# Linear-attention layers of a fused four-stack transformer: whole layers written out, and the second MLP layer moved by one pass

## The reference, cut to what matters

```python
for i in range(8):                       # layers
    residual = x
    Q  = _feature_map(einsum('nsd,hdk->nshk', x, Wq[i]) + bq[i])   # elu(.) + 1
    Kf = _feature_map(einsum('nsd,hdk->nshk', x, Wk[i]) + bk[i])
    V  = einsum('nsd,hdk->nshk', x, Wv[i]) + bv[i]
    KV, sumK = sum(Kf * V, axis=1), sum(Kf, axis=1)
    Z = 1.0 / (Q * sumK[:, None] + 1e-06)
    att = (Q * KV[:, None] * Z).reshape(n, s, 16 * 64)
    x = _layer_norm(gelu(att @ Wo[i] + bo[i]) + residual, ln1_s[i], ln1_b[i])
    residual = x
    h = gelu(x @ W1[i] + b1[i])          # 128 -> 512
    h = gelu(h @ W2[i] + b2[i])          # 512 -> 128
    x = _layer_norm(h + residual, ln2_s[i], ln2_b[i])
```

## Time and profile before

| | |
|---|---|
| median of three runs | 5932.04 us |
| lowest, highest | 5924.21, 5944.2 us |
| profiled execution, its own time | 5937.09 us |
| its span, first to last instruction | 5935.3 us |
| busy over the span: TensorE, VectorE, ScalarE, GpSimd | 80%, 64%, 50%, 19% |
| the linear-attention layers in it | from 1393 to about 4318 us |
| TensorE's mean granted clock | 0.893 of full speed |

### The profile page before, as it was taken

One profiled execution on the slowest core, in us unless ns is written; L12 is line 12 of the kernel. 1 busy time (PEld: TensorE's weight loads), 2 busy tenths in 40 slices (PEclk: granted clock), 3 DMA queues, 4 the chain that ended last, 5 costly groups with the idle time before them and its releaser, 6 DMA issues.

```text
span 5935.3 us, 74341 instructions
## 1 busy us (share of the span) xinstructions
PE 4747.4 (80%) x19788; PEld 2813.9 (47%) x19788; DVE 3781.6 (64%) x11596; ACT 2983.3 (50%) x5234; POOL 1115.9 (19%) x1520
## 2 busy tenths in 40 slices
PE   4778888866888888888888888888858745999964
PEld 2667777753333333333333333333335533666643
DVE  4445554467776767667666776777665674556576
ACT  1010000015887878778787787878712212555531
POOL 1100000021222222222222222222220002333310
PEclk9888888878999999999999999999979966989976
DMA  1000000000000000000000000000000000110100
GB/s 47 1 1 1 1 1 1 1 1 18 0 15 4 6 13 1 15 4 10 9 1 18 0 11 7 1 18 0 0 0 0 0 0 22 37 40 35 43 1 14
DMA packets 96397, 59.02 MB, mean 10 GB/s; under 512 B 58809, under 2 KB 91278, under 8 KB 93604
## 3 DMA queue, kind: packets, MB, share of 16 engines
q1 hardware_dynamic: 88436, 42.52, 2.7%
q10 hardware_dynamic: 7600, 12.58, 0.6%
HBM read 46.49 MB, written 8.61 MB: 9 GB/s over the span
## 4 chain that ended last, share of the span: by engine, by line
PE 49%; DVE 24%; issue 12%; ACT 8%; DMA 2%; POOL 1%; DVEq 1%; ACTq 1%; SPq 1%; POOLq 0%
PE bank L1493 7%; PE bank L1526 4%; PE bank L1507 4%; PE bank L1215 3%; DVE arena L1657 3%; DVE arena L1643 3%; PE bank L1520 3%; PE bank L2163 3%; PE bank L1212 3%; DVE arena L1626 2%; PE bank L1204 2%; DMA packed_dram<-arena 2%; DVE arena L1282 2%; DVE arena L1668 2%; PE bank L2196 2%
## 5 line engine op out<-in xcount | busy, mean ns | idle before, releaser
L1493 PE MATMUL bank<-arena 128*128 (+1 forms) x3072 | 1478.9, 619 | 12.9 <-ACT arena L1555 11.3
L1493 PEld LDWEIGHTS bank<-arena 128*128 128x128 f32 x3072 | 601.2, 200 | 745.4 <-issue 713.1
L1626 DVE SCALAR_TENSOR_TENSOR arena<-arena 128x256 f32<-128x256 f32 x1024 | 390.5, 418 | 777.7 <-ACT arena L1555 773.1
L1507 PE MATMUL bank<-arena 128*128 128x512 f32 x1024 | 565.4, 635 | 219.6 <-DVE arena L1657 218.2
L1568 ACT ACTIVATE arena<-arena,const_table 128x256 f32<-128x256 f32 x1024 | 558.6, 600 | 78.7 <-POOL arena L1695 78.6
L1695 POOL TENSOR_SCALAR arena<-arena 128x512 f32<-128x512 f32 x512 | 317.9, 621 | 1353.9 <-DVE arena L1637 1346.6
L1643 DVE SCALAR_TENSOR_TENSOR arena<-bank,bv,arena 128x256 f32<-128x256 f32 x1024 | 450.0, 476 | 0.0
L1657 DVE SCALAR_TENSOR_TENSOR arena<-arena 128x256 f32<-128x256 f32 x1024 | 447.6, 478 | 0.7 <-issue 0.7
L1507 PEld LDWEIGHTS bank<-arena 128*128 128x128 f32 x1024 | 168.6, 191 | 556.3 <-DVE arena L1657 499.2
L1554 ACT ACTIVATE arena<-bank,bqk 128x512 f32<-128x512 f32 x512 | 350.3, 684 | 159.5 <-PE bank L1493 126.2
L1637 DVE SCALAR_TENSOR_TENSOR arena<-bank,bqk,arena 128x512 f32<-128x512 f32 x512 | 384.1, 750 | 18.0
(11 more groups left out here) (350 smaller groups left out, 8804.6 us busy)
## 6 DMA issues: line engine op xcount, KB each, us to landing
arena<-packed_dram SPq DMA_DIRECT2D x48, 192.0 KB
arena<-packed_dram ACTq DMA_DIRECT2D x16, 576.0 KB
arena<-in_L_attn_Wk_dram SPq DMA_DIRECT2D x16, 256.0 KB, 3.2
arena<-in_L_attn_Wq_dram SPq DMA_DIRECT2D x16, 256.0 KB, 3.9
arena<-in_L_attn_Wv_dram SPq DMA_DIRECT2D x16, 256.0 KB, 4.4
arena<-in_L_attn_Wo_dram SPq DMA_DIRECT2D x8, 512.0 KB, 3.8
arena<-in_L_attn_W_dram SPq DMA_DIRECT2D x16, 256.0 KB, 3.0
packed_dram<-arena SPq DMA_DIRECT2D x16, 192.0 KB, 2.1
```

Source lines behind the costliest of these rows:

```text
L1493: nc.tensor.matmul(bank[:, RING1[m % 5], :], w1p[k][:, i * P:(i + 1) * P], zT_of(g), start=True, stop=True).then_inc(a1_proj.sem, 1)
L1507: nc.tensor.matmul(bank[:, 6, :], wo1[:, i, :], a1_att[:, i % 4, :], start=(i == 0), stop=(i == NB1 - 1)).then_inc(a1_outd.sem, 1)
L1626: last = nc.vector.scalar_tensor_tensor(seqs(a1_kf[:, i % 2, :])[q], seqs(a1_ek[:, i % 2, :])[q], 1.0, seqs(a1_kf[:, i % 2, :])[q], ALU.mi ...
```

## The change

In `over_layers` the loop over pairs of slots goes: all eight slots of a layer are written out, the loop over layers 1 to 7 stays, `opening` is left once a layer, and the drain has three slots. There are four hooks, in slots 0 to 3: the biases of y, of h and x1, and of h2 and ln2 are copied apart. W1 and W2 are loaded apart, each when its own last product is done.

The MLP is cut in two. `h_pe` (lag 2, at w = 3) makes the four products with W1 into banks 0, 1, 6 and 0. The products with W2 (`h2_pe`) go to the next slot (lag 3), two at w = 0 and two at w = 1, into bank 1; their gelu `h2_act` (lag 3) is the first of the gelu window, which is now at w = 3. The second norm has lag 3 with its steps at w = 4 to 6, the first norm has its transposes in at w = 5, statistics at w = 6, normalisation at w = 7 and its transposes back in the next slot at w = 0 (lag 2).

`out_pe`, `inv_act` and `att_dve` come one block later (w - 4, w - 2, w - 3), `query_pool` stands at w, and gpsimd sums the second residual ahead of the first. `a1_ek`, `a1_eq`, `a1_kf` have three buffers, `a1_x1` two, and `a1_fin` shares the memory of `a1_h`.

```diff
     def one_layer(layer, low):
         parts = parts_of(layer)
         opening()
-        for s in range(2):
-            hooks[s](layer)
+        for s in range(G):
+            if s < len(hooks):
+                hooks[s](layer)
             slot(parts, s, low, G)
-        hooks[2](layer)
-        with eng.Fori(0, (G - 2) // 2) as j:
-            opening()
-            for v in range(2):
-                for lag, fn in parts:
-                    fn(2 * j + (2 + v - lag), (v - lag) % 2)
...
+            HBANK = (0, 1, 6, 0)
...
                             a1_y_act.wait(nc.tensor, t - 1)
-                            a1_h2_act.wait(nc.tensor, t - 2)
+                            if not before_all(g, 2):
+                                a1_h_act.wait(nc.tensor, t - 2, 3)
...
-                def mlp_pe(g, u):
+                def h_pe(g, u):
                     t = turn(g)
+                    nc.tensor.wait_ge(a1_w1_loaded, 16 * weights_of(g))
                     a1_x1d.wait(nc.tensor, t)
                     for i in range(NF1):
+                        if i == 1:
+                            a1_h2_act.wait(nc.tensor, t - 1)
+                        if i == 2:
+                            if isinstance(g, int) and g == G - 1:
+                                a1_y_act.wait(nc.tensor, t)
+                            else:
+                                a1_y_act.wait(nc.tensor, t + 1)
+                        if i == 3:
+                            a1_h_act.wait(nc.tensor, t, 1)
+                        nc.tensor.matmul(bank[:, HBANK[i], :], w1a[:, i * P:(i + 1) * P], a1_x1[:, u, :],
                                          start=True, stop=True).then_inc(a1_h_psum.sem, 1)
...
+                def h2_pe(half):
+                    def fn(g, u):
+                        t = turn(g)
+                        if half == 0:
+                            nc.tensor.wait_ge(a1_w2_loaded, 16 * weights_of(g))
+                            a1_h_act.wait(nc.tensor, t)
+                            a1_zt.wait(nc.tensor, t - 1)
+                        for i in range(half * NF1 // 2, (half + 1) * NF1 // 2):
+                            last = nc.tensor.matmul(bank[:, 1, :], w1b[:, i, :], a1_h[:, i, :],
+                                                    start=(i == 0), stop=(i == NF1 - 1))
...
                 for w in range(NB1):
                     pe.append((0, proj_pe(w)))
-                    of(pe, out_pe, w - 3)
+                    of(pe, out_pe, w - 4)
                     act.append((0, exp_act(w)))
-                    of(act, inv_act, w - 1)
+                    of(act, inv_act, w - 2)
                     dve.append((0, feature_dve(w)))
-                    of(dve, att_dve, w - 2)
-                    of(pool, query_pool, w - 1)
-                    if w == 2:
-                        pe.append((2, mlp_pe))
-                        act += [(1, gelu_table_act), (1, y_act), (2, h_act), (1, exp_table_act)]
-                        pool += [(1, residual_pool(0)), (2, residual_pool(1))]
+                    of(dve, att_dve, w - 3)
+                    of(pool, query_pool, w)
+                    if w == 0:
+                        pe += [(2, turn_back_pe(0)), (3, h2_pe(0))]
+                        act.append((2, back_act(0)))
+                    if w == 1:
+                        pe.append((3, h2_pe(1)))
                     if w == 3:
-                        pe += [(1, turn_in_pe(0)), (2, turn_in_pe(1))]
-                        dve += [(1, norm_stats_dve(0)), (2, norm_stats_dve(1))]
+                        pe.append((2, h_pe))
+                        act += [(1, gelu_table_act), (3, h2_act), (1, y_act), (2, h_act), (1, exp_table_act)]
+                        pool += [(3, residual_pool(1)), (1, residual_pool(0))]
                     if w == 4:
-                        pool += [(1, norm_rstd_pool(0)), (2, norm_rstd_pool(1))]
+                        pe.append((3, turn_in_pe(1)))
+                        dve.append((3, norm_stats_dve(1)))
+                        pool.append((3, norm_rstd_pool(1)))
                     if w == 5:
-                        dve += [(1, norm_dve(0)), (2, norm_dve(1))]
+                        pe.append((1, turn_in_pe(0)))
+                        dve.append((3, norm_dve(1)))
                     if w == 6:
-                        pe += [(1, turn_back_pe(0)), (2, turn_back_pe(1))]
-                        act += [(1, back_act(0)), (2, back_act(1))]
+                        pe.append((3, turn_back_pe(1)))
+                        act.append((3, back_act(1)))
+                        dve.append((1, norm_stats_dve(0)))
+                        pool.append((1, norm_rstd_pool(0)))
+                    if w == 7:
+                        dve.append((1, norm_dve(0)))
```

More of the change, by code:

```diff
@@ L39 @@
 C_ALL = C_HEAD + 16
-ARENA = 25728
+ARENA = 26752
 def host_table():
@@ L159, in over_layers @@
     opening()
-    for s in range(G, G + 2):
+    for s in range(G, G + 3):
         slot(parts, s, 0, G)
@@ L1464, in one_layer @@
                     if not first:
+                        a1_h_psum.wait(sp, layer * G - 1)
+                    sp.dma_start(w1a[:], one("W1").rearrange("l d f -> d (l f)")).then_inc(a1_w1_loaded, 16)
+                    if not first:
                         a1_h2_psum.wait(sp, layer * G - 1)
-                    sp.dma_start(w1a[:], one("W1").rearrange("l d f -> d (l f)")).then_inc(a1_mlp_loaded, 16)
                     sp.dma_start(w1b[:], one("W2").rearrange("l (b p) d -> p (l b) d", p=P))\
-                        .then_inc(a1_mlp_loaded, 16)
+                        .then_inc(a1_w2_loaded, 16)
                 if n:
@@ L1509, in out_pe, with weights_of, before_all @@
                     return fn
-                def mlp_pe(g, u):
+                def weights_of(g):
+                    return layer if isinstance(g, int) and g < 0 else layer + 1
+                def before_all(g, back):
+                    return isinstance(layer, int) and layer == 0 and isinstance(g, int) and g < back
+                def h_pe(g, u):
                     t = turn(g)
-                    before = isinstance(g, int) and g < 0
-                    nc.tensor.wait_ge(a1_mlp_loaded, 32 * (layer if before else layer + 1))
+                    nc.tensor.wait_ge(a1_w1_loaded, 16 * weights_of(g))
@@ L1530, in turn_in_pe @@
                 def turn_in_pe(i):
                     def fn(g, u):
-                        lns[i]["in"].wait(nc.tensor, turn(g))
+                        t = turn(g)
+                        lns[i]["in"].wait(nc.tensor, t)
+                        if i == 0 and not before_all(g, 1):
+                            a1_h_act.wait(nc.tensor, t - 1)
+                        if i == 1 and not (isinstance(g, int) and g == G - 1):
+                            a1_h_act.wait(nc.tensor, t + 1, 2)
                         for q in range(QT):
@@ L1592, in h_act, with h2_act @@
                             a1_h2_psum.wait_free(nc.scalar, t)
-                        nc.scalar.activation(a1_h[:, i, :], bank[:, i % 2, :], ACT.Gelu_apprx_tanh,
+                        nc.scalar.activation(a1_h[:, i, :], bank[:, HBANK[i], :], ACT.Gelu_apprx_tanh,
                                              bias=b11[:, i:i + 1]).then_inc(a1_h_act.sem, 1)
+                def h2_act(g, u):
+                    t = turn(g)
                     a1_h2_psum.wait(nc.scalar, t)
-                    lns[1]["in"].wait_free(nc.scalar, t)
-                    nc.scalar.activation(a1_g2[:], bank[:, 6, :], ACT.Gelu_apprx_tanh, bias=bd1[:, 3:4])\
+                    lns[1]["in"].wait(nc.scalar, t - 1)
+                    nc.scalar.activation(a1_g2[:], bank[:, 1, :], ACT.Gelu_apprx_tanh, bias=bd1[:, 3:4])\
                         .then_inc(a1_h2_act.sem, 1)
```

71 lines of the change are left out of this document (38 added, 33 removed).

## The result

| | before | after |
|---|---|---|
| median (lowest to highest) | 5928.5 us (5924.21 to 5944.2) | 5870.38 us (5866.52 to 5872.23) |
| ratio, 95% interval | | 0.9896 (0.9877 to 0.9916) |
| profiled execution, its span | 5937.09, 5935.3 us | 5872.23, 5870.4 us |
| TensorE's mean granted clock | 0.893 | 0.901 |

The change gains 58 us by the medians and 65 between the two profiled executions. The prediction said 5855, with a range of 5765 to 5930, and a gain of 77.

A forecast was written before the change was run, and what follows sets the result against it. Hand-overs bound the kernel, no engine being full: window, VectorE's catching up, transposes back, ScalarE's remaining blocks. Layers gain 76 us, layer 0 4, the drain costs 3.4, total 77: 5860 profiled, 5855 median predicted, range 5765 to 5930.

The forecast's parts named there:

- Clean turn: Time between gelu window openings without a clock drop: 42.4 us, only 0.5 under the 42.86 of before.
- window: ScalarE's gelu load to the exponential load's end: shrinks from 10.07 to 6.9 us as the wait for W2 goes.
- VectorE's stretch: VectorE after the window: four blocks, two statistics, two normalisations without pause, 19.0 us, ending at 27.1.
- The drop: TensorE's half clock after the 2.3 us wait before h1: costs 1.8 us, in three turns of four; taken as +1.3.
- clock drops in each turn: Rival: TensorE's clock falls in every turn, 60 x 0.5 = 30 us less gain, 5885; no separate chance given.
- Once a layer: Layer opening: four bias hooks cost 0.4 us each, and VectorE's idleness at the jump back adds 2.9 in slot 0.
- The drain: Pipeline's end: one slot and one leftover block more, costing 3.4 us, bounds 0 and 10.
- Reloads and jumps: Layer's pair loop: 24 of 33 exponential reloads go, 1.2 us each in a turn; removed inner jumps give nothing.
- it doesn't do what it says: the reloads only, 5903: Rival: the MLP's stall stays and only the reloads gain, about 29 us; partial gain (5895 to 5914) 0.14.
- The rule on jumps: Skill's fetch stall on taken branches: 16 removed inner jumps would give 55 us more; denied for the short jump.
- Instruction supply, the slower case: Rival: refills in straight-line layer code stall ScalarE or VectorE 3 us each, 5950; slower 0.13, supply or chain.
- Buffers and lags: Third exponential buffer and longer lags remove ScalarE's waits for gpsimd's query step, none on the chain: nothing.

The follow-up runs named there:

- experiment 3: After, with the four products with W2 moved from the next slot's w = 0 and 1 to w = 7 of the same slot: 5739.74 us.
- experiment 2: After, with two more 512-column products, whose result nobody reads, on TensorE ahead of the wait before h1: 5801.62 us.
- Experiments 8: Before, with its loops over pairs of slots kept and the 24 exponential-table reloads in them taken out: 5906.59 us.
- experiment 9: Before, with whole layers written out in the old order, but the exponential table still reloaded at slots 2, 4 and 6: 5928.63 us.
- Experiment 6: After, with two exponential buffers instead of three and ScalarE's wait for VectorE one block earlier: 5850.11 us.
- experiment 4: After, with block 4's three projections placed between h0 and h1 on TensorE: 5788.93 us.
- experiment 1: Before, in its own order of work, with all eight slots of a layer written out and 24 reloads gone: 5874.11 us.
- experiment 5: After, with the exponential table reloaded at slots 2, 4 and 6 of each layer: 5859.62 us.

## Why the prediction was right, and where it was not

The direction, the chain and the length of its links held. The account of where the gain comes from did not: it named the right places but gave the reload what belonged to the jump, and it left the drain at a third of what it costs.

- **Clean turn, window, VectorE's stretch.** Forecast 42.4, 6.9 and 19.0 us; measured 42.60, 6.92 and 19.2. That 3.2 us of a shorter window would come back through W2's 3.4 us behind the transposes back was the point of the working, and experiment 3 shows it from the other side: with W2 out of that stretch, 1.4 us a turn come at once.
- **The drop.** Its price was forecast as 1.8 us in three turns of four. The price is 1.6 to 1.7, shown by experiment 2. Over the whole layer the share was right, 44 of 56 turns, but not its places: in slots 4 to 7 it fell on 26 of 28, the rival "clock drops in each turn", so they took 44.2 each and not 43.7, 2.0 us a layer more. In slots 1 to 3 it fell on only 11 of 21.
- **Once a layer.** Slots 1 to 3 together were forecast as 132.3 and took 131.9. The hooks show longer waits (up to 4.7 us each, in place of the 1.70 of the earlier trace rows), and, as worked out, nearly all of it is covered: without a drop these slots take 43.05 to 43.13 in experiment 2, against 42.60, so a hook costs 0.5 and not 0.4. That the sum fits is partly luck, since fewer drops made up for it. Slot 0 was forecast as 47.0 and took 45.8: I let VectorE's jump add its 2.9, but VectorE's idle time there shrank, from 17.7 us in six jumps to 5.6. Why it did wasn't tested. The two misses cancel the drop's in slots 4 to 7: 354.5 for a layer against 354.1. To that extent the fit is luck.
- **The layer before** was taken as 365.05, one layer; the mean is 364.7. With layer 0 (5.3, forecast 4) and the last turn's 2.1 the layers gave 78.5 of the forecast 80.
- **The drain** is the term that was mis-sized: 3.4 forecast, with bounds of 0 and 10, and 10.6 measured, outside them. TensorE and ScalarE at the end of after:

```profile
4231.54 0.69 ACT L1618 ACTIVATE arena<-bank,b 128x512 f32<-128x512 f32 x1 [0.17 <-PE bank L1532]
4237.58 0.78 ACT L1642 ACTIVATE arena<-bank,bd 128x512 f32<-128x512 f32 x1 [5.35 <-PE bank L1568]
```

```profile
4238.50 5.63 PE L1543 MATMUL bank<-arena 128*128 128x512 f32 x8 [1.04 <-ACT arena L1642]
```

The last group's h is complete at 4232.2, but its product with W2 waits until 4238.50, since it waits for the second norm of the group before (the wait on `a1_zt` in `h2_pe`). The wait is not new: in before it stood ahead of the products with W1. But that norm now runs one slot later, and its result is written 33.3 us behind the last opening, against 19.4. I had counted slots and not looked for a wait that only bites when nothing fills it. This is read from the traces; no run took the wait away, for experiment 3 left it in place. With the 2.55 us of the later first window, which the sum left out, this is why the gain is 65 and not 77 by the profiled executions. The measured medians are 7 us closer together still: the profiled execution of before lies 8.6 over the median of its runs, that of after only 1.9, and I had taken 5 for both.

- **Reloads and jumps.** I priced 24 reloads at 1.2 us and the inner jumps at nothing, because ScalarE's table load stands idle by issue only six times. That reading failed. It asked one engine, and VectorE was the one that stood still at the jump, its idle time put down to ScalarE. Experiments 8 and 9 show what is behind the number: 1.17 us for a jump, 0.90 for a reload, each covering the other. The sum of 29 us was nevertheless too small, for the two together free 51: some 16 in the turns at loop heads (14 x 1.17), some 13 in slot 2 (1.9 x 7), some 16 in turns that no longer drop (in slots 3 to 7 11 of 35 do, where before has at least 21), and 4 at the layer's crossing. What stopped the ten drops, no run shows. The rival "it doesn't do what it says: the reloads only, 5903" thus fails by its number, though not by its kind: the order by itself adds 4 us to what writing out gives, less than the two intervals can tell apart.
- **The rule on jumps.** The Trainium skill (Runtime: NRT & Kernel Launch, Instruction fetch mechanics) says that an engine stalls on a fetch after a taken branch whose target isn't in its current window. The trace shows VectorE's 16 gaps at the jumps, though not that a fetch fills them, and so agrees for the inner loop as well as for the outer one, which my prediction denied. It doesn't agree with the price that I worked out under it from the outer jump: 1.28 us, not 3.4.
- **Instruction supply, the slower case.** Not seen. Inside the written-out layers VectorE has seven stalls by issue of at most 0.2 us, besides those at the jump back; one of 2.7 us stands where the drain begins. The turn of 43.32 us that I had held against this rival was no evidence: it runs from slot 2 to slot 3 of layer 0, which in before lie in the first pass of the loop over pairs, and not in written-out code.
- **Buffers and lags: nothing.** Experiment 6 shows it for the buffers. The lags by themselves were not tried.

What decided the size of the result is a thing between the two bounds that I had given: the new order, with the clock kept up, is worth some 70 us on top of writing out (5874 for that alone, which has drops of its own, and 5802), and the half clock behind one 2.2 us wait, right inside the gelu window, takes nearly all of them back.

## What to carry to other kernels

Before a reload, a jump or a wait is priced at a place where several stand together, look at that place on every engine: the record names only the one that ended last, and taking it away may show the next, of the same length. Where TensorE waits a microsecond or two once a turn, look at the length of the products behind the wait before its own length, and at whether another engine waits for them: work put in front of it, even work that nobody reads, may be worth more than the wait. And price a longer pipeline's drain by following its waits with nothing else in flight, not by its number of slots.

## What the runs showed of the hardware

- A wait of 2.20 us on TensorE is followed by slower 512-column products in most turns and not in others of the same kernel (4.19 and 2.84 us for three, above). In experiment 3 the same wait, 62 times, mostly has no such effect. Two more products in front of it, and a wait of 0.5, left none of the 49 turns in slots 1 to 7 of layers 1 to 7 with the drop: 1.7 us of added work bought 69 us in all.
- What a stretch at half clock costs hangs on where it falls: mostly 1.6 to 1.7 us of the turn when it starts 2 to 4 us behind the opening of the gelu window (after), 0.01 at 11 to 13 us (42.70 against 42.69, experiment 4), 0.1 to 0.3 at 21 to 22 us (experiment 1).
- A jump back costs each engine its own time, at its own place: in the loop over pairs 1.28 us on VectorE, 16 times of 16, and nothing on record on ScalarE; at the loop over layers 3.3 us on ScalarE (19.9 in six, after) and on VectorE 3.0 before (17.7 in six) and 0.9 after.
- A table load of 1.28 us is worth 0.90 on the chain in the old order (experiment 9), nothing where a jump of 1.17 covers it, nothing in the new order (experiment 5), and 2.6 behind a hook, some of it the clock's. The following activation starts 1.29 us after the load's start, as at 3338.09 and 3339.38 above.
